# Causal attention on one core: the own-key score block moves to its own PSUM bank, VectorE pre-writes the causal masks there, and two normalisations move to GpSimd

## What is computed

```python
# 16 heads, key size 8, value size 64; T = 256
h = layernorm(x)
q, k, v = split_heads(h @ Wq), split_heads(h @ Wk), split_heads(h @ Wv)
scores = einsum('bhqd,bhkd->bhqk', q, k) / sqrt(8)
scores = where(triu(ones((T, T)), k=1), -inf, scores)      # causal
attn = softmax(scores, axis=-1)
x = x + concat_heads(attn @ v) @ Wo
h = layernorm(x)
# 8 experts, each takes its 64 best tokens of each row of the batch
probs = softmax(h @ gate_w)
out = sum over experts of scatter(top_p * (gelu(h[top] @ w1) @ w2))
x = x + out
```

## Time and profile before

| | |
|---|---|
| median of 3 runs | 616.21 us (615.49 to 616.58) |
| the profiled execution | 615.37 us, span from first to last instruction 613.6 us |
| attention | about 0 to 436 us, experts after it |
| PE, PEld, DVE, ACT, POOL busy | 89%, 71%, 61%, 64%, 42% of the span |
| mean granted TensorE clock | 0.975 of full speed, 1.00 throughout attention |

### The profile page before, as it was taken

How to read it: one execution, slowest core, us unless ns; L and a number is a source line. 1 busy time by engine, 2 the same in 40 slices (tenths; PEclk the granted TensorE clock), 3 DMA queues, 4 the chain that set the end, 5 groups by cost and what they waited for, 6 DMA issues and landing times. The chain is left out here.

```text
span 613.6 us, 14118 instructions
## 1 busy us (share of the span) xinstructions
PE 545.6 (89%) x4836; PEld 435.5 (71%) x4836; DVE 373.9 (61%) x951; ACT 393.1 (64%) x1370; POOL 257.9 (42%) x247
## 2 busy tenths in 40 slices
PE   1379999999999999999999999998218999999996
PEld 1246768778777787777776877777216998989896
DVE  4357686776866867768677686674665334443244
ACT  2289797887978878889778797892306442433330
POOL 7256464654654646436455464462420111101111
PEclk9999999999999999999999999999758999999998
DMA  4865252240422513315224042700011001000001
GB/s 135 216 169 181 66 138 64 77 134 18 126 69 67 137 39 98 106 31 137 66 70 133 21 120 69 206 2 1 1 39 50 18 19 36 10 19 18 19 19 44
DMA packets 49659, 45.82 MB, mean 75 GB/s; under 512 B 4176, under 2 KB 46416, under 8 KB 49616
## 3 DMA queue, kind: packets, MB, share of 16 engines
q1 hardware_dynamic: 49040, 44.73, 26.5%
q10 hardware_dynamic: 576, 0.52, 0.3%
HBM read 26.35 MB, written 18.89 MB: 74 GB/s over the span
## 5 line engine op out<-in xcount | busy, mean ns | idle before, releaser
L366 ACT ACTIVATE prob<-s_ps,neg_max 128x128 f32<-128x128 f32 (+1 forms) x512 | 209.8, 436 | 22.0 <-DVE neg_max L515 19.6
L331 POOL TENSOR_TENSOR probn<-prob,inv 128x512 f32<-128x512 f32 x64 | 66.7, 1041 | 169.6 <-PE t_ps L628 158.0
L350 POOL TENSOR_TENSOR probn<-prob,inv 128x1024 f32<-128x1024 f32 x64 | 121.3, 1895 | 16.3 <-DVE inv L526 15.9
L366 ACT ACTIVATION_READ_ACCUMULATOR prob<-s_ps,neg_max 128x1 f32 x512 | 113.3, 221 | 0.0
L596 PE MATMUL ctx_ps<-probT,v_sb 128*64 128x256 f32 (+1 forms) x1024 | 97.3, 332 | 0.9 <-DVE probT L512 0.9
L453 DVE TENSOR_REDUCE neg_max<-s_ps 128x4 f32<-128x1024 f32 x64 | 77.0, 1203 | 24.8 <-PE s_ps L562 24.6
L596 PEld LDWEIGHTS ctx_ps<-probT,v_sb 128*64 128x64 f32 x1024 | 63.6, 136 | 30.0 <-issue 11.6
L802 POOL TENSOR_TENSOR y_parts<-y_sb,y_parts 128x512 fp32r<-128x512 f32 x16 | 20.6, 1286 | 137.8 <-ACT y_parts L818 137.8
L512 DVE COPY probT<-t_ps 128x512 f32<-128x512 f32 x64 | 44.2, 691 | 43.1 <-PE t_ps L628 42.9
L578 PE MATMUL t_ps<-ident,probn 128*128 128x128 f32 x256 | 61.3, 280 | 5.4 <-ACT probT L411 4.0
L542 PE MATMUL misc_ps<-wo_sb,ctxT 128*128 128x128 f32 x512 | 63.5, 278 | 0.8 <-DVE ctxT L508 0.8
(11 more groups left out here) (145 smaller groups left out, 1051.4 us busy)
## 6 DMA issues: line engine op xcount, KB each, us to landing
qT<-q_rows SPq DMA_DIRECT2D x16, 512.0 KB, 4.0
q_rows<-qk_hi SPq DMA_DIRECT2D x32, 128.0 KB, 2.4
q_rows<-qk_lo SPq DMA_DIRECT2D x32, 128.0 KB, 2.4
k_diag_even<-k_rows SPq DMA_DIRECT2D x32, 128.0 KB, 4.2
k_diag_odd<-k_rows SPq DMA_DIRECT2D x32, 128.0 KB, 4.3
k_rows<-qk_hi SPq DMA_DIRECT2D x30, 128.0 KB, 2.4
k_rows<-qk_lo SPq DMA_DIRECT2D x30, 128.0 KB, 2.4
w_raw<-in_L_ffn_w SPq DMA_DIRECT2D x1, 2048.0 KB, 10.6
```

The source lines that it names most:

```text
L331: nc.gpsimd.tensor_tensor(probn[r][:, 0:HG * P].rearrange("p (i k) -> p i k", i=HG), prob[r][:, 0:HG * P].rearrange("p (i k) -> p i k", i=HG),
L350: nc.gpsimd.tensor_tensor(probn[r][:, HG * P:].rearrange("p (i k) -> p i k", i=HG), prob[r][:, HG * P:].rearrange("p (i k) -> p i k", i=HG ...
L366: last = nc.scalar.activation(prob[r][:, first + i * keys:first + (i + 1) * keys], scores[:, i, :], ACT.Exp, bias=neg_max[:, r, block_, i: ...
```

## The change

Four things, in the order of the diff:

- `s1_ps` becomes `[P, 2, HG, P]`: the first 128 keys of all four heads lie in one bank, the own 128 keys in the other. Each bank gets one full-height product of 512 columns. The four products with half tables and the tables are gone; so is the mask product of `s0_ps`. The very first unit alone lays the mask down with TensorE.
- VectorE copies `causal` (bfloat16, broadcast over four heads) into `s0_ps` after `exp0` of the unit ahead, and into the own-key bank of `s1_ps` after `exp1` of the unit ahead. The products then add onto it. TensorE waits for `filled0` and `filled1`.
- Both normalisations are two GpSimd instructions each (subtract, wait, multiply), and `xg_lo` is on GpSimd as well. The second reciprocal of a unit now stands ahead of the maximum of the next `s0_ps`.
- The exponentials and the maximum of `s1_ps` read it through a rearranged pattern.

```diff
-        s1_ps = ps("s1_ps", [P, HG, T])
+        s1_ps = ps("s1_ps", [P, 2, HG, P])
...
+            def norm(dst, src, mv, rstd, centered, count, done):
+                nc.gpsimd.tensor_tensor(dst[:, :, :], src, bcast(mv[:, :, 0], 2, D), ALU.subtract).then_inc(centered, 1)
+                pool.wait_ge(centered, count)
+                nc.gpsimd.tensor_tensor(dst[:, :, :], dst[:, :, :], bcast(rstd[:, :], 2, D), ALU.mult).then_inc(done, 1)
...
-                        if isinstance(b, int) and b == -2:
-                            zeros_and_masks()
...
+                    if j == 0 and has(b - 2, B):
+                        pool.wait_ge(rstd2_done, b - 1)
+                        await_count(pool, x2T_done, b - 2)
+                        await_count(pool, xg_lo_done, b - 2)
+                        norm(xn2, x_all[:, bass.ds((b - 2) * TB, TB), :], mv2, rstd2, xn2_centered, b - 1, xn2_ready)
+                    if j == 1 and has(b + 2, B):
+                        pool.wait_ge(rstd1_done, b + 3)
+                        await_count(pool, xT_done, b + 2)
+                        norm(xn1, x_all[:, bass.ds((b + 2) * TB, TB), :], mv1, rstd1, xn1_centered, b + 3, xn1_ready)
+                        if isinstance(b, int) and b == -2:
+                            zero_keys()
+                    if j == 3 and has(b - 2, B):
+                        pool.wait_ge(xg_hi_done, b - 1)
...
                     if has(u + 1, UNITS):
                         dve.wait_ge(exp0, u + 2)
                         nc.vector.reciprocal(inv[:, r1, 0, :], sums[:, r1, 0, :]).then_inc(inv0, 1)
+                    if has(u + 2, UNITS) and has(u + 1, UNITS):
+                        nc.vector.tensor_copy(s0_ps[:, :, :], bcast(causal[:, :], 1, HG)).then_inc(filled0, 1)
...
                         nc.vector.tensor_copy(probT[rm][:, 1024:1536], t_ps[rm][:, :]).then_inc(t_dve, 1)
+                    if has(u + 1, UNITS):
+                        dve.wait_ge(exp1, u + 2)
+                        if has(u + 2, UNITS):
+                            nc.vector.tensor_copy(s1_ps[:, 1, :, :], bcast(causal[:, :], 1, HG)).then_inc(filled1, 1)
+                        nc.vector.reciprocal(inv[:, r1, 1, :], sums[:, r1, 1, :]).then_inc(inv1, 1)
                     if has(u + 2, UNITS):
                         dve.wait_ge(s0_done, u + 3)
                         nc.vector.tensor_reduce(out=neg_max[:, r2, 0, :], in_=s0_ps[:, :, :], axis=AX.X,
...
-                    if has(u + 1, UNITS):
-                        dve.wait_ge(exp1, u + 2)
-                        nc.vector.reciprocal(inv[:, r1, 1, :], sums[:, r1, 1, :]).then_inc(inv1, 1)
...
+                        await_count(pe, exp1, u + 1)
+                        nc.tensor.matmul(s1_ps[:, 0, :, :], qT[kb][:, q, P:T], k_diag[kb][:, q, :, 0:P], start=True, stop=True)
+                        await_count(pe, filled1, u + 1)
                         if isinstance(u, int) and u == -1:
-                            pe.wait_ge(halves, 10)
...
+                            nc.tensor.matmul(s1_ps[:, 1, :, :], ident_bf[:, :], bcast(causal[:, :], 1, HG), start=True, stop=True)
+                        last = nc.tensor.matmul(s1_ps[:, 1, :, :], qT[kb][:, q, P:T], k_diag[kb][:, q, :, P:T],
+                                                start=False, stop=True, skip_group_check=True)
                         last.then_inc(s1_done, 1)
...
-                        await_count(pe, exp0, u + 2)
-                        nc.tensor.matmul(s0_ps[:, :, :], qT[kb][:, q, 0:P], k_diag[kb][:, q, :, 0:P], start=True, stop=False)
-                        nc.tensor.matmul(s0_ps[:, :, :], ident_bf[:, :], bcast(causal[:, :], 1, HG),
-                                         start=False, stop=True).then_inc(s0_done, 1)
+                        await_count(pe, filled0, u + 2)
+                        if isinstance(u, int) and u == -2:
+                            nc.tensor.matmul(s0_ps[:, :, :], ident_bf[:, :], bcast(causal[:, :], 1, HG), start=True, stop=True)
+                        nc.tensor.matmul(s0_ps[:, :, :], qT[kb][:, q, 0:P], k_diag[kb][:, q, :, 0:P], start=False, stop=True,
+                                         skip_group_check=True).then_inc(s0_done, 1)
```

More of the change, by code:

```diff
@@ L289, in _, with zero_keys @@
                                     base=0, pattern=[[-1, P]], channel_multiplier=1).then_inc(consts2, 1)
-            def zeros_and_masks():
+            def zero_keys():
                 nc.gpsimd.memset(f32(k_diag[0][:, :, :, :]), 0.0).then_inc(zeroed, 1)
[L294 to L321, removed]
@@ L365, in exps @@
                 for i in range(HG):
+                    to = prob[r][:, first + i * keys:first + (i + 1) * keys]
                     last = nc.scalar.activation(
-                        prob[r][:, first + i * keys:first + (i + 1) * keys], scores[:, i, :], ACT.Exp,
+                        to if keys == P else to.rearrange("p (k t) -> p k t", k=2), scores(i), ACT.Exp,
                         bias=neg_max[:, r, block_, i:i + 1], accum_out=sums[:, r, block_, i:i + 1])
@@ L387, in batch @@
                         act.wait_ge(max1, u + 2)
-                        exps(r1, 1, s1_ps, T, HG * P, exp1)
+                        exps(r1, 1, lambda i: s1_ps[:, :, i, :], T, HG * P, exp1)
                     if j == 3 and has(b + 2, B):
@@ L431, in norm_stats @@
                 last.then_inc(stats_done, 1)
[L433 to L437, removed]
             def split_qk_weights():
@@ L452, in batch @@
                         dve.wait_ge(s1_done, u + 2)
-                        nc.vector.tensor_reduce(out=neg_max[:, r1, 1, :], in_=s1_ps[:, :, :], axis=AX.X,
+                        nc.vector.tensor_reduce(out=neg_max[:, r1, 1, :], in_=s1_ps[:, :, :, :].rearrange("p k i t -> p i k t"), axis=AX.XY,
                                                 op=ALU.max, negate=True).then_inc(max1, 1)
@@ L551, in batch @@
                         q, kb = (j + 1) % G, par if j < 3 else 1 - par
+                        await_count(pe, exp1, u + 1)
+                        nc.tensor.matmul(s1_ps[:, 0, :, :], qT[kb][:, q, P:T], k_diag[kb][:, q, :, 0:P], start=True, stop=True)
+                        await_count(pe, filled1, u + 1)
                         if isinstance(u, int) and u == -1:
-                            pe.wait_ge(halves, 10)
-                        await_count(pe, exp1, u + 1)
-                        tiles = ((slice(0, HALF), 0), (slice(HALF, P), 2))
-                        for rows, i in tiles:
-                            nc.tensor.matmul(s1_ps[:, i:i + 2, :], qT[kb][rows, q, P:T], k_diag[kb][rows, q, i:i + 2, :],
-                                             start=True, stop=False, skip_group_check=True)
-                        for half in range(2):
-                            cols = slice(P + half * HALF, P + (half + 1) * HALF)
-                            for rows, i in tiles:
-                                last = nc.tensor.matmul(s1_ps[:, i:i + 2, cols], half_rows[rows, half, :],
-                                                        bcast(half_masks[rows, half, :], 1, 2),
-                                                        start=False, stop=(half == 1), skip_group_check=True)
+                            nc.tensor.matmul(s1_ps[:, 1, :, :], ident_bf[:, :], bcast(causal[:, :], 1, HG), start=True, stop=True)
+                        last = nc.tensor.matmul(s1_ps[:, 1, :, :], qT[kb][:, q, P:T], k_diag[kb][:, q, :, P:T],
+                                                start=False, stop=True, skip_group_check=True)
                         last.then_inc(s1_done, 1)
```

31 lines of the change are left out of this document (10 added, 21 removed).

## The result

The changed kernel takes **625.85 us** (median of 4, 624.81 to 626.85) against 616.3 of the kernel before beside it; the ratio is 1.0164, with a 95% interval of 1.0146 to 1.0182. It is slower by about 9.6 us.

A forecast was written before the change was run, and what follows sets the result against it. Attention was held by a latency ring through TensorE, VectorE and ScalarE, with TensorE nearly full. Terms 15.4 - 2.4 + 2.5 + 0.7 = +16.2 on 615.4 gave 631.6, stated as 632 us; range 622 to 642.

The forecast's parts named there:

- the ring: Attention, every step: last transposes, VectorE's copy, own-key bank write, last score product, back to last transposes; 5.52 us.
- the rival of a faster write: VectorE's own-key bank write takes 0.43 us, not 0.69; about 620, up to 627; slower but under +11 had 0.15.
- The old ring: Attention before the change: TensorE, VectorE and ScalarE in turn, 10.24 us per two steps; forecast to become 5.47 a step.
- The batch: Four steady attention steps: 5.78 + 5.52 + 5.52 + 9.12 = 25.94 us against 24.91, +1.03; +15.4 over 15.
- The long step: Attention step with output projection and query and key products: only the 0.23 us mask product won, 9.35 to 9.12.
- the passage from j = 3 to 0: Attention step where VectorE also does statistics and normalisation work: VectorE's chain leads, 5.78 us.
- The start: Before attention: normalisation on GpSimd lets TensorE begin at about 6.4 instead of 8.83 us, -2.4.
- The first units: First attention units, TensorE waiting for exponentials: +2.0 for two steps, +0.8 at first j = 3, -0.3 mask; +2.5 us.
- the third ring: Attention: own-key write waits for `exp1`, then reciprocal, maximum and exponentials follow; new, 5.41 us a step.
- The end: End of attention: the last normalisation stands alone on the path, 1.3 us on GpSimd for 0.60, +0.7.
- VectorE as the bound in every step: Attention rival: VectorE bounds every step, or product weights are exposed; 26.8 us a batch, about 645; over +21 had 0.18.
- The faster case: Attention rival: write done before TensorE asks, short steps stay 5.12 us, -0.43 a batch; 608 us, chance 0.06.

The follow-up runs named there:

- the pair of runs with the added instruction: Changed kernel plus one 512-element VectorE instruction a unit, ahead of the own-key bank write (651.5 us) or behind the maximum of `s0_ps` (632.7 us).
- the second added instruction: Changed kernel plus one 512-element VectorE instruction a unit behind the maximum of `s0_ps`: 632.7 us, ratio 1.0269.

## Why the prediction was right, and where it was off

**The mechanism.** Right, and shown: the pair of runs with the added instruction tells the ring from the load, and leaving the write out (with the early reciprocal) turns the loss into a gain. TensorE's wait stands at three of four steps with VectorE's write as releaser; the ring of 5.52 measured 5.53 to 5.56 in the middle steps.

**The number.** +16.2 was forecast on the profiled execution and its span grew by 9.4. The direction and the range held, the middle of the forecast did not: +9.6 falls into "slower but under +11", which had a chance of 0.15, and 625.85 even lies in the 620 to 627 that the rival of a faster write spans. By the time alone that rival could not be told from the forecast; the length of the write and the steps of 5.53 to 5.56, where it had 5.34, tell them apart.

**The old ring.** Its sum, 10.24 against 10.24 in the trace, proves nothing by itself: its parts follow each other without a gap from 200.77 to 211.01, so they have to add up. What speaks for it are the waits at its links; no run changed one of its links alone.

**The write's length.** Taken as 0.69 from rows of the same size; measured 0.684 on average over 63. "The write is fast" falls by that row: VectorE's write of 512 elements from 16-bit data into PSUM took what its 32-bit instructions of that size take, not the 0.43 of the rival. The Trainium skill, "VectorE: DVE Perf Modes", section "What auto-detection actually checks", has the doubled rate either for 16-bit tensors throughout or with source and destination both in SBUF. This write is neither, and the 684 ns agree.

**The batch.** +1.03 forecast, +0.65 measured (25.56 against 24.91), which over 15 batches is 5.7 us, most of the miss. (Counted over the whole stretch, from the seventh copy of `probT` to the last, the growth is 10.1 us for the 15.4 forecast.) Two terms were mis-sized. The long step was 8.82, not 9.12: I had priced the two forms of `s1_ps` alike, and around the half-height form more time passes. Of the 0.53 that the step lost, 0.23 is the s0 mask; 0.17 is the distance from the transposes to the first product of `s1_ps` (0.31 before, 0.14 after), and 0.11 the half of the projection behind it (1.89 from 219.88 to 221.77 before, 1.78 from 223.00 to 224.78 after). That it goes with the form and not with VectorE's writes, the run with two banks and TensorE's masks shows: its three products of `s1_ps` take 0.78 (216.71 to 217.49) where the half-height form takes 0.56 (219.32 to 219.88), and its long step is still 0.05 under 9.35. What in the form costs the time no run separates. The trace of before has the weight load of the first half-height product start only with the product, 0.17 after the load ahead of it ended (219.15 to 219.32), with no releaser that the profile names. And the passage from j = 3 to 0 was 5.65, not 5.78, since VectorE's instructions stood a little closer.

**The start.** -2.4 forecast; TensorE's first instruction came 2.57 earlier and its first scores 3.33. The reason, VectorE held by GpSimd's clearing, is shown by the 7.02 beside two clearings. The 0.76 beyond 2.57 arose in the transfers between: from the first store to the first load 5.12 us (10.23 to 15.35) after 5.35 (12.80 to 18.15), and from there to the first product 6.66 after 7.19. Why they were faster stays open.

**The first units.** +2.5 forecast, and the total came out near that by parts that did not. From the first scores, 3.33 early, to the seventh copy of `probT` (76.13 against 77.28, 1.15 early), where the steady batches begin, the loss was 2.2. The two steps that I had put at +2.0 by the third ring grew by 1.1 (29.58 to 39.50 between first products of `s1_ps`, 9.92 for 8.81), and the rest, put at +0.5, was 1.1 as well.

**The end.** +0.7 forecast, +0.5 measured (the last gate values at 445.73 against 436.24, 9.49 later, with 8.96 of it already there at the last copy of `probT`). GpSimd had room for its new work, as forecast.

**The rivals.** VectorE as the bound in every step is refuted by the second added instruction; its ceilings of 0.85 for the write and 0.2 for the hop by 0.684 and 0.05. The faster case is refuted: in the short steps the write was never ready when TensorE asked; only in the long one was it, as forecast.

## What to carry to other kernels

An engine that is 98% busy is not yet the bound: add up the ring of waits that returns to the same instruction, and put a moved instruction's length into every ring that passes its place. The same 0.5 us instruction cost 25 us in the ring and 7 behind it. When a change has several parts, price the place of each: here two parts gained 3 us each, and the third, which stood between the last transposes and the next product, lost more than both. A sum that covers a stretch of the trace without a gap always comes out right; a ring is shown by what happens when one of its links is made longer.

## What the runs showed of the hardware that I had not expected

VectorE's normalisation of two 128x128 tiles, 0.60 on its own, took 3.71 beside one clearing of 3.51 on GpSimd and 7.02 beside two in succession: one of its two instructions took 6.95, so it did not get its turn between the clearings. Around a half-height product pair with its masks TensorE took 0.17 more in front and 0.11 more behind than around full-height products. A bfloat16 write into PSUM as float32 took 684 ns for 512 elements, as long as a copy that reads PSUM (690).
